# Cross-attention kernel: 17 instead of 18 products per context piece, q loaded from ScalarE's queue, two steps of the prologue exchanged

## The reference, cut to what matters

```python
query = hidden_states @ Wq              # 100 x 640
keyt  = enc @ Wk                        # 718 x 640
valt  = enc @ Wv
hs    = _mha(query, keyt, valt)         # 8 heads of 80, softmax over 718 keys
ca_q1 = jnp.einsum('btc,th->bch', ca, Wq_ca)[:, indices, :]
ca_hs1 = _mha(ca_q1, residual, residual)
ca_hs2 = _mha(ca_hs1 @ Wq, ca @ Wk_ca, ca @ Wv_ca)
out = (hs + ca_hs2) @ Wout + b_out + residual
```

## Time and profile before

| | |
|---|---|
| median of 3 runs | 1001.76 us (997.12 to 1004.11) |
| profiled execution | 1004.24 us, span 1002.5 us |
| PE busy | 985.5 us, 98% of the span |
| DVE, ACT, POOL busy | 652.0, 490.8, 342.9 us |
| mean granted TensorE clock | 0.992 of full speed |
| main DMA queue | 75.6% of 16 engines' span |

### The profile page before, as it was taken

The page is one execution under the profiler, slowest core; times in us unless marked ns, Lnnn a source line. Parts: engine busy times, 40 slices in busy tenths (PEclk is TensorE's granted clock), DMA queues, the critical chain, the costliest instruction groups (busy, mean ns, idle before and its releaser), DMA issues.

```text
span 1002.5 us, 20727 instructions
## 1 busy us (share of the span) xinstructions
PE 985.5 (98%) x6740; PEld 964.2 (96%) x6740; DVE 652.0 (65%) x1129; ACT 490.8 (49%) x895; POOL 342.9 (34%) x286
## 2 busy tenths in 40 slices
PE   9989999999999999999999999999999999998998
PEld 8989889999999999999999999999999999997997
DVE  6544676667667766667676767676766666667444
ACT  7524555555554546464636364636464545446110
POOL 5212253434252516161515243333333333416000
PEclk9979999999999999999999999999999999999999
DMA  7959978797879797979797979788887878795354
GB/s 264 307 192 257 266 190 210 166 202 168 191 172 195 171 187 177 187 181 185 181 182 185 181 184 181 191 171 202 170 201 162 210 162 193 171 213 152 98 181 146
DMA packets 154169, 190.12 MB, mean 190 GB/s; under 512 B 80928, under 2 KB 108192, under 8 KB 154144
## 3 DMA queue, kind: packets, MB, share of 16 engines
q1 hardware_dynamic: 147456, 177.44, 75.6%
q10 hardware_dynamic: 6688, 12.35, 3.7%
HBM read 81.56 MB, written 19.95 MB: 101 GB/s over the span
## 4 chain that ended last, share of the span: by engine, by line
PE 85%; DVE 5%; SPq 4%; DMA 3%; ACT 2%; issue 1%; ACTq 0%; DVEq 0%
PE psS L744 21%; PE psB L779 20%; PE psB L784 10%; PE psS L719 7%; PE psT L760 6%; PE psS L888 6%; PE psT L806 4%; PE psT L812 2%; SPq L382 2%; DMA encT_raw<-in_encT_dram 1%; PE psB L861 1%; SPq L379 1%; PE psB L838 1%; PE psT L813 1%; PE psS L944 1%
## 5 line engine op out<-in xcount | busy, mean ns | idle before, releaser
L744 PE MATMUL psS<-encT_keep,Wk_keep 128*128 128x360 f32 x1440 | 253.7, 329 | 0.0
L744 PEld LDWEIGHTS psS<-encT_keep,Wk_keep 128*128 128x128 f32 x1440 | 237.3, 188 | 0.9 <-issue 0.2
L779 PE MATMUL psB<-PT_h,encN_h 120*128 120x400 f32 x576 | 202.3, 351 | 0.0
L779 PE MATMUL psB<-PT_l,encN_h 120*128 120x400 f32 x576 | 198.8, 345 | 0.0
L1130 ACT ACTIVATE probs<-psS,negmax 100x718 f32<-100x718 f32 x128 | 110.2, 861 | 129.2 <-DVE negmax L1522 129.0
L606 POOL TENSOR_TENSOR encT_keep<-encT_raw,encT_keep 128x718 fp32r<-128x718 f32 x45 | 79.7, 1771 | 181.6 <-ACT encT_keep L1159 179.3
L1546 DVE TENSOR_TENSOR kT<-psS,kT 128x718 fp32r<-128x718 f32 x80 | 72.4, 905 | 94.9 <-ACT kT L1154 94.7
L614 POOL TENSOR_TENSOR encN_l<-enc_raw,encN_h 120x768 fp32r<-120x768 f32 x48 | 92.6, 1930 | 91.4 <-ACT encN_h L1166 90.0
L597 POOL TENSOR_TENSOR Mbd<-Mbd,fmask 128x320 fp32r<-128x320 f32 x48 | 45.8, 954 | 226.7 <-DMA Mbd<-m_split 224.1
L784 PE MATMUL psB<-PT_h,encN_l 120*128 120x400 f32 x576 | 120.4, 344 | 0.7 <-POOL encN_l L614 0.7
L1154 ACT ACTIVATE kT<-psS 128x718 fp32r<-128x718 f32 x80 | 61.7, 771 | 115.2 <-PE psS L744 110.0
(11 more groups left out here) (245 smaller groups left out, 1643.5 us busy)
## 6 DMA issues: line engine op xcount, KB each, us to landing
kstack<-kT SPq DMA_DIRECT2D x64, 448.8 KB
kstack<-kT SPq DMA_DIRECT2D x192, 112.2 KB
enc_raw<-in_encN_dram SPq DMA_DIRECT2D x48, 360.0 KB, 5.6
encT_raw<-in_encT_dram SPq DMA_DIRECT2D x45, 359.0 KB, 6.4
kstack<-kT SPq DMA_DIRECT2D x32, 359.0 KB
kstack<-kT SPq DMA_DIRECT2D x32, 269.2 KB
kstack<-kT SPq DMA_DIRECT2D x32, 179.5 KB, 3.6
kstack<-kT SPq DMA_DIRECT2D x64, 89.8 KB, 3.5
```

Source lines behind the costliest of these rows:

```text
L744: mm = pe.matmul(keys_in(f, first)[:, half, 0:HALF], w[:, c, f * 128:(f + 1) * 128], e[:, c, k0:k0 + HALF], start=(j == 0), stop=(j == 3 * ...
L779: pe.matmul(psB[:, 1, 0:RH], eN[0][:, k, cc], PT[p][:, k, rows], start=(k == 0 and p == 0), stop=False)
```

## The change

It has three parts.

**The stacked last tile.** KP becomes 128: five full tiles of keys (FULLK = 5) and a tail of 78. The tail's three products would use 78 of 128 rows each; now they are 2 matmuls of TSTK = 117 rows. Rows 0 to 77 hold high x high in the one and high x low in the other, rows 78 to 116 hold in each one half (39 keys) of low x high. For this:
- `norm` scales 39 columns of P a second time into the columns behind the 718 (one more VectorE instruction per head), so that the transpose puts them into rows 78 to 116;
- `enc_twice` on ScalarE writes the tail's high part into the low operand too;
- `enc_low` on GpSimd is four instructions instead of three, the tail's low part is made in place in `enc_raw` (`tail_low`);
- `tail_enc` (two DMAs on SyncE's queue), `tail_pt0` (one there) and `tail_pt1` (one on ScalarE's) copy 39 rows each to rows 78 to 116;
- the transposes, the PT evictions and the context loads work on 128 instead of 120 rows, and the parts of the context come in the order tiles 4 and 5, 0 and 1, 2 and 3.

**q.** The next batch's `load_q` is issued by ScalarE, after `pt_high(i,4)`, and no longer by SyncE between `lift(i+1,0)` and `lift(i+1,1)`.

**The prologue.** M's heads 6 and 7 are loaded, and split on ScalarE and VectorE, ahead of batch 0's context.

```diff
-KP = (KEYS + KT - 1) // KT
+KP = 128
@@ sync
+                sp.wait_ge(s["hlo"], 6)
+                load_heads(6, 2)
                 sp.wait_ge(s["wlo"], 5)
                 sp.dma_start(enc0_raw, encT[0].rearrange("(c p) k -> p c k", p=128)).then_inc(s["encin"], 16)
-                sp.wait_ge(s["hlo"], 6)
-                load_heads(6, 2)
...
+                def tail_pt0(b):
+
+                    wait_apart(sp, s["ptlo"], HEADS * b + 4, s["passed_sp"])
+                    sp.dma_start(raw(PT[1][TAIL:TSTK, FULLK, 0:RH]), raw(PT[0][TH:TAIL, FULLK, 0:RH]))\
+                      .then_inc(s["pttail"], 16)
+
+                def tail_enc(b):
+
+                    wait_apart(sp, s["encN"], LOWS * b + 1, s["passed_sp"])
+                    for p in range(2):
+                        sp.dma_start(raw(eN[p][TAIL:TSTK, FULLK, :]), raw(tail_low[p * TH:(p + 1) * TH, :]))\
+                          .then_inc(s["entail"], 16)
@@ tensor, context
-                    for k in range(KT):
+                    for k in range(FULLK):
                         for p in range(2):
                             pe.matmul(psB[:, 1, 0:RH], eN[0][:, k, cc], PT[p][:, k, rows],
                                       start=(k == 0 and p == 0), stop=False)
-                    for k in range(KT):
-                        if u == 0 and k % KQ == 0:
-                            pe.wait_ge(s["encN"], PARTS * i + k // KQ + 1)
-                        mm = pe.matmul(psB[:, 1, 0:RH], eN[1][:, k, cc], PT[0][:, k, rows],
-                                       start=False, stop=(k == KT - 1))
-                    mm.then_inc(s["u"], 1)
+                    for n, k in enumerate((4, 0, 1, 2, 3)):
+                        if u == 0 and n in (0, 1, 3):
+                            pe.wait_ge(s["encN"], LOWS * i + (n + 1) // 2 + 2)
+                        pe.matmul(psB[:, 1, 0:RH], eN[1][:, k, cc], PT[0][:, k, rows], start=False, stop=False)
+                    if u == 0:
+                        pe.wait_ge(s["entail"], 32 * i + 32)
+                    if c == 0:
+                        pe.wait_ge(s["pttail"], 32 * i + 16 * half + 16)
+                    pe.matmul(psB[:, 1, 0:RH], eN[0][0:TSTK, FULLK, cc], PT[0][0:TSTK, FULLK, rows],
+                              start=False, stop=False)
+                    pe.matmul(psB[:, 1, 0:RH], eN[1][0:TSTK, FULLK, cc], PT[1][0:TSTK, FULLK, rows],
+                              start=False, stop=True).then_inc(s["u"], 1)
@@ scalar, batch
                     pt_high(i, 4, first)
+                    if not last:
+                        act.wait_ge(s["scores"], HEADS * (i + 1))
+                        load_q(act, i + 1)
                     expo(i, 7)
...
-                for c in range(CT):
-                    enc0_high(c)
                 head_high(6)
                 q_high(1, 3)
                 head_high(7)
                 q_high(1, 4)
+                for c in range(CT):
+                    enc0_high(c)
@@ vector, norm
                     nc.vector.reciprocal(inv[:, h:h + 1], total[:, h:h + 1]).then_inc(s["inv"], 1)
-                    dve.wait_ge(s["inv"], HEADS * i + h + 1)
+                    dve.wait_ge(s["inv"], 2 * (HEADS * i + h) + 1)
+                    nc.vector.tensor_scalar(P[h % PRING][0:S, KEYS:KEYS + TH],
+                                            P[h % PRING][0:S, FULLK * KP:FULLK * KP + TH], inv[:, h:h + 1],
+                                            None, ALU.mult).then_inc(s["inv"], 1)
+                    dve.wait_ge(s["inv"], 2 * (HEADS * i + h) + 2)
                     nc.vector.tensor_scalar(P[h % PRING][0:S, 0:KEYS], P[h % PRING][0:S, 0:KEYS], inv[:, h:h + 1],
                                             None, ALU.mult).then_inc(s["norm"], 1)
```

More of the change, by code:

```diff
@@ L29 @@
 KT = 6
-KP = (KEYS + KT - 1) // KT
+KP = 128
 KPAD = KT * KP
-HALF = KPAD // 2
+HALF = 360
+FULLK = KEYS // KP
+TAIL = KEYS - FULLK * KP
+TH = TAIL // 2
+TSTK = TAIL + TH
 RH = R // 2
@@ L256, in program @@
         stage1_stores = "qst0 qst1 qst2 qst3a qst3b v2st mst0 mst1 mst2"
[L257 removed]
+        names = " ".join((loads, products_done, exps_and_highs, steps_and_lows, splits, tails, stage1_loads, stage1,
                           stage1_stores)).split()
@@ L272, in wait_lifted, with third @@
                     eng.wait_ge(s_lift[key], 16 * LIFTS[key] * batches)
+        def third(c):
+            return slice(4, 6) if c == 0 else slice(2 * (c - 1), 2 * c)
         score_slot = [0, 1, 1, 0, 0, 1, 0, 0]
@@ L327, in free @@
                         wait_apart(sp, s[name], n, s["passed_sp"])
-                def load_q(b, first=False):
-                    free("scores", HEADS * b, first)
-                    for p in range(2):
-                        q3 = q_d[p].rearrange("(h d) n -> d h n", d=D)[:, :, bass.ds(b * S, S)]
-                        sp.dma_start(raw(qst[p][0:D, :, :]), raw(q3)).then_inc(s["qin"], 16)
-                        qh = q_d[0].rearrange("(h d) n -> d h n", d=D)[p * EX:(p + 1) * EX, :, bass.ds(b * S, S)]
-                        sp.dma_start(raw(qst[p][D:STK, :, :]), raw(qh)).then_inc(s["qin"], 16)
                 def load_encT(b, c, first=False):
@@ L362, in load_enc @@
                 def load_enc(b, c, first=False):
-                    free("encN", PARTS * (b - 1) + c + 1, first)
-                    ks = slice(c * KQ, (c + 1) * KQ)
+                    free("encN", LOWS * (b - 1) + c + 2, first)
+                    if c == 0:
+                        free("entail", 32 * b, first)
+                    ks = third(c)
                     sp.dma_start(rawN[:, ks, :], encN[bass.ds(b, 1)].rearrange("o (k p) c -> p (o k) c", p=KP)[:, ks, :])\
@@ L517, in batch @@
                         sp.dma_start(wv_raw, tiled(Wv)).then_inc(s["wvin"], 16)
-                        load_q(i + 1)
-                    else:
+                    tail_pt0(i)
+                    tail_enc(i)
+                    if not first:
                         wait_apart(sp, s["hsp"], 2 * i, s["passed_sp"])
@@ L525, in batch @@
                         lift(i + 1, 0)
-                        if not first:
-                            load_q(i + 1)
                         lift(i + 1, 1)
@@ L541, in _ @@
                 batch(B - 1, last=True)
-                sp.wait_ge(s["encN"], PARTS * B)
+                sp.wait_ge(s["encN"], LOWS * B)
                 for t in range(2):
@@ L610, in enc_low @@
                 def enc_low(b):
-                    for c in range(PARTS):
-                        ks = slice(c * KQ, (c + 1) * KQ)
-                        pool.wait_ge(s["encNhi"], PARTS * b + c + 1)
+                    pool.wait_ge(s["encNhi"], LOWS * b + 2)
+                    nc.gpsimd.tensor_tensor(tail_low, rawN[:, FULLK, :], eN[0][:, FULLK, :],
+                                            ALU.subtract).then_inc(s["encN"], 1)
+                    pool.wait_ge(s["encN"], LOWS * b + 1)
+                    nc.gpsimd.tensor_tensor(eN[1][:, FULLK - 1, :], rawN[:, FULLK - 1, :], eN[0][:, FULLK - 1, :],
+                                            ALU.subtract).then_inc(s["encN"], 1)
+                    pool.wait_ge(s["encN"], LOWS * b + 2)
+                    for c in range(1, PARTS):
+                        ks = third(c)
+                        pool.wait_ge(s["encNhi"], LOWS * b + c + 2)
                         nc.gpsimd.tensor_tensor(eN[1][:, ks, :], rawN[:, ks, :], eN[0][:, ks, :],
                                                 ALU.subtract).then_inc(s["encN"], 1)
-                        pool.wait_ge(s["encN"], PARTS * b + c + 1)
+                        pool.wait_ge(s["encN"], LOWS * b + c + 2)
                 def spread_v2(b):
@@ L692, in wo_low @@
                     pool.wait_ge(s["wolo"], c + 1)
-                for c in range(3):
+                for c in range(2):
                     wo_low(c)
                 enc_low(B - 1)
-                for c in range(3, FT):
+                for c in range(2, FT):
                     wo_low(c)
@@ L1346, in batch @@
                         enc_high(i, 0)
+                        enc_twice(i)
                     if last:
@@ L1392, in batch @@
                     pt_high(i, 7)
-                    if not last:
+                    if last:
+                        tail_pt1(i)
+                    else:
                         u_high(i, 1)
+                        tail_pt1(i)
                         expo(i + 1, 0)
@@ L1805, in _ @@
                 q_low(1, 2)
-                for c in range(CT):
-                    enc0_low(c)
                 head_low(6)
@@ L1811, in _ @@
                 q_low(1, 4)
+                for c in range(CT):
+                    enc0_low(c)
                 q_low(1, FT)
```

24 lines of the change are left out of this document (20 added, 4 removed).

## The result

The changed kernel takes 1030.01 us (median of 4, 1022.15 to 1038.56) where the kernel before took 999.57 on the same chip (997.12 to 1004.11): ratio 1.0273, 95% interval 1.0192 to 1.0354. The kernel is slower; that it is slower by more than 2% is likely, but the interval doesn't settle it. The forecast was 985 us, so it missed by 45 us and had the wrong sign. The profiled execution of the changed kernel, 1038.56 us, was the slowest of the four and in the slower of the two states that executions fall into: the ratio is taken from the means of the other three (1027.4 us), and the batches read from the profile can be some 0.7 us longer than theirs (11 us over 16 batches).

The account below looks back on a forecast made before the run. TensorE, busy for 985.5 of 1002.5 us, was taken as the bound; terms of -27.0 + 10.0 = -17.0 us took the profiled 1004.24 to 987.2, or 985 us on the median's scale, range 975 to 1000.

Parts of the forecast that it names:

- Step 7: q loads on ScalarE, tail copies on SyncE, enc_twice and GpSimd's fourth instruction: all claimed to cost nothing.
- Step 1: TensorE's products: six fewer in each of 16 batches at 0.183 us each, -17.6 us at most.
- step 5: Transposes' weight loads: stationary part grows from 120 to 128 columns, +2.8 us (0 to 4).
- Step 2: Prologue: splitting heads 6 and 7 ahead of the context removes TensorE's 3.1 us stop and slow stretch, -9.4 us.
- Rival B: Prologue: batch 0's context, 3.2 us later, becomes the next 3 us stop, nothing gained; 994 us, chance 0.16.
- Steps 3, 4 and 6: +3.0 at values(i-1,0) from later norm; +1.4 at turn(i,6) for PT's low part; +2.8 for norm waits in batches 0, 15.
- Rival C: norm(i,3) loses its gap to GpSimd, context(i-1,5) stands 1.6 us in 14 batches; 1008 us, chance 0.10.
- Rival A: Whole kernel: VectorE instruction and GpSimd's timing cost nothing, products and prologue gain in full; 978 us, chance 0.14.
- rival D: Tail copies land late behind the context loads, context(i,0) waits some 1.3 us x 15; 1004 us, chance 0.08.

Follow-up runs that it names:

- the fastest version: Changed kernel with q loads back on SyncE, PT's tail copy on ScalarE, and ScalarE making the 39 columns instead of VectorE's extra instruction: 994.04 us, ratio 0.9919.

## Why the prediction was wrong, step by step

**Step 7 failed**, and with it the sign. It put the q loads and the tail copies "at nothing". The q loads were judged by ScalarE's 2.18 us of idle time before `expo(i,7)`, and in the changed kernel that part held: the issues took 2.0 to 2.3 us, and `expo(i,7)` waited for "issue" three times, 9.6 us in all. What I never asked is what q's 750 KB run beside. I had moved them on paper from one queue to another, and looked at the two issuing engines; the transfer that they now meet is `lift(i+1,0)`, and its landing releases a buffer that ScalarE, then VectorE, then TensorE want. The trace of before would have shown this: `k_high(i+1,2)` waits only 2.28 us, and for TensorE, so that a lift later than that would be what it waits for. The step's last sentence, "If v2 and the lift behind them slip by a microsecond, nobody waits yet", was wrong too: even with q back on SyncE, where ScalarE waits for the lift in no batch, `scores` waits for q and the lift, and one tail copy's issue, 0.8 us, was worth 6.6 us. Together, q 24 us and that copy 7, these are 31 of the 45 us between forecast and measurement.

Step 1 (products, -17.6) and step 5 (transposes, +2.8): right. The median batch of 51.01 us in the fastest version and the 141 ns show both, as far as a batch goes; some of the products' gain has not arrived in the whole time (below). The Trainium skill's columns / 1.2 ns (TensorE: Matmul & The Clock Gate, section LDWEIGHTS) would be 6.7 ns for the eight columns; the trace has 4, as its two rows of before gave.

Step 2 (prologue, -9.4): the mechanism was right, the size wrong: 3.1 and 4.2 us in two comparisons. The stop and its slow clock were read from one profiled execution and priced as if every execution had them; in one other TensorE lost that time earlier, and there was no stop, in three more the stop was 1.4 to 1.8 us. Rival B did not occur.

Steps 3, 4 and 6 (+3.0, +1.4, +2.8, the VectorE instruction, with a share of GpSimd's timing): the instruction alone measured 7.5, close to their sum of 7.2. But the parts are off: 0.28 us and not 0.19 per instruction, and the cost lies with batches 0 and 15 (3.8 us each, 1.1 of it from Wout's load, where 2.8 in all were forecast) and ahead of them, while the steady batch, 0.3 us longer in the mean, pays about what steps 3 and 4 said (4 us of 4.4). All this is from one profiled execution; that the sum comes close is in part luck.

Rival C: at `norm(i,3)` it did not occur. At 492.06 the new row took 0.39 us in place of 0.25, `norm` followed at 492.49 with 0.59 (0.60 in all loop batches, 0.74 before), and it was GpSimd's next instruction, at 492.57, that took 2.11 us. At `norm(i,6)`, the second place that the rival named, its mechanism did occur, in all 14 loop batches: the scaling took 2.06 us in place of 0.60, beside a GpSimd instruction that had begun before it (503.89 + 1.85). The kernel before, then the changed one:

```profile
493.15 0.60 DVE L1529 TENSOR_SCALAR probs<-probs,inv 100x718 f32<-100x718 f32 x1
504.07 2.06 DVE L1590 TENSOR_SCALAR probs<-probs,inv 100x718 f32<-100x718 f32 x1
506.22 0.91 DVE L1607 TENSOR_TENSOR kT<-psS,kT 128x718 fp32r<-128x718 f32 x1
```

It cost nothing in this batch, because VectorE had been idle for 1.89 us at this place: `k_low` still starts as soon as ScalarE is done with the high part (505.42 + 0.77), and TensorE is busy for all of the 27 us from 485 to 512. Rival A is what the median batch does once q, one copy and the VectorE instruction are mended. The wait of rival D did not occur in the changed kernel but did in two experiments, for another reason and at three times its price.

The sum again, from what was measured: -17.6 + 2.8 + 7.5 - 3.1 = -10.4; with q +24 and one tail copy +7 it is +21 where +27 was measured. Some 6 us are open. The fastest version leaves more: -17.6 + 2.8 - 3.1 = -17.9 was to be had without the VectorE instruction, and -8.1 was measured, so that some 10 us are open there. They can lie in the two tail copies that remain on SyncE, in ScalarE's added instruction, and in the batches of 51.6 to 52.6 us that this version still has (0.4 us a batch in the mean, 5 to 6 us in all); none of this was tried.

## What to carry to other kernels

A transfer that is moved to another queue meets other transfers. Before it counts as free, list what is in flight at that moment, which buffer each of these releases and by how much its waiter is early; here a lift that landed 3 us later cost 3 to 4 us in each of 14 batches. A small instruction or an 0.8 us issue on a queue that runs just in time is priced by the slack behind it, not by its length. And a stop seen in one execution is a bound on what removing it gives: look for it in a second profile before it is counted in full.
